# Unread products in the inverse's slots, three trees' bias gathers moved beside the delta rule, tiles added home in two of three segments

## The reference

```python
for _ in range(DEPTH):                       # 8 levels, 256 leaves
    logit = jnp.einsum('bsd,bsd->bs', x, nw[node]) + nb[node]
    node = 2 * node + 1 + (logit > 0).astype(jnp.int32)
leaf = node - NN
h = act(jnp.einsum('bsd,bsdl->bsl', x, w1[leaf]) + b1[leaf])
return jnp.einsum('bsl,bsld->bsd', h, w2[leaf]) + b2[leaf]
```

## Time and profile before

| | |
|---|---|
| median of 3 runs | 4053.92 us (4050.29 to 4074.92) |
| profiled execution: its time, its span | 4069.24 us, 4067.5 us |
| PE busy, over the span | 3332.8 us (82%) |
| DVE, ACT, POOL busy | 2154.1, 1386.8, 918.9 us |
| granted clock of PE, mean over the span | 0.841 |
| PE on the chain that ended last | 64% |
| transfers | 274.44 MB, mean 67 GB/s |

### The profile page before, as it was taken

How to read it: one execution, slowest core, us unless ns; L and a number is a source line. 1 busy time by engine, 2 the same in 40 slices (tenths; PEclk the granted TensorE clock), 3 DMA queues, 4 the chain that set the end, 5 groups by cost and what they waited for, 6 DMA issues and landing times.

```text
span 4067.5 us, 86528 instructions
## 1 busy us (share of the span) xinstructions
PE 3332.8 (82%) x35358; PEld 2395.5 (59%) x35358; DVE 2154.1 (53%) x4781; ACT 1386.8 (34%) x3193; POOL 918.9 (23%) x988
## 2 busy tenths in 40 slices
PE   3488888788887888887676679767599999999998
PEld 3356666566775666666566557556355455545554
DVE  4457677466677566675244345423344554455444
ACT  1344443344344343442033232113144333333331
POOL 0011111411111311113155642345211111101110
PEclk6688897688787888986588889888688999999989
DMA  4201101201001200102174623375310111010000
GB/s 143 101 18 39 34 18 28 99 28 33 28 23 44 89 28 23 34 18 68 43 237 142 199 98 104 111 232 185 136 32 22 42 39 40 22 42 27 16 17 16
DMA packets 202180, 274.44 MB, mean 67 GB/s; under 512 B 33344, under 2 KB 145728, under 8 KB 201408
## 3 DMA queue, kind: packets, MB, share of 16 engines
q1 hardware_dynamic: 174784, 210.04, 16.3%
q0 software_dynamic: 18432, 50.49, 3.5%
...
...
## 4 chain that ended last, share of the span: by engine, by line
PE 64%; DVE 15%; issue 6%; ACT 5%; DMA 3%; another core or an unknown queue 2%; POOL 1%; SPq 0%; DVEq 0%; ACTq 0%; POOLq 0%
PE banks L531 5%; PE banks L2810 5%; DVE s_d_kq L624 3%; PE banks L1781 3%; PE banks L2382 3%; PE banks L1790 2%; PE banks L766 2%; PE banks L2624 2%; PE banks L2366 2%; PE banks L1192 2%; PE banks L755 2%; PE banks L921 2%; PE banks L2394 2%; PE banks L935 2%
## 5 line engine op out<-in xcount | busy, mean ns | idle before, releaser
L531 PE MATMUL banks<-s_d_xT,s_w_qkvg 128*128 128x512 f32 x640 | 353.2, 679 | 30.9 <-DMA s_d_xT<-xnT 21.1
L624 DVE SCALAR_TENSOR_TENSOR s_d_kq<-banks,s_conv_w,s_d_kq 128x511 f32<-128x511 f32 (+2 forms) x384 | 285.7, 745 | 48.5 <-ACT s_d_kq L576 36.9
L2496 ACT ACTIVATE s_g_pT<-banks 128x1536 f32<-128x1536 f32 (+1 forms) x96 | 153.0, 1594 | 436.1 <-PE banks L2384 436.1
L2460 DVE TENSOR_REDUCE s_g_nmax<-banks 128x4 f32<-128x512 f32 (+3 forms) x128 | 187.9, 1489 | 175.5 <-PE banks L2368 175.5
L2810 PE MATMUL banks<-s_m_we,s_m_tT 128*128 128x512 f32 x512 | 233.9, 602 | 3.5 <-DVE s_m_x L2873 3.2
L1781 PEld LDWEIGHTS banks<-s_q_xsT,s_q_w 128*128 128x128 f32 x1008 | 171.7, 216 | 65.0 <-issue 47.0
L1790 PE MATMUL banks<-s_q_w,s_q_hm 128*128 (+1 forms) x504 | 178.7, 442 | 34.5 <-DVE s_q_hm L1834 18.3
L1781 PE MATMUL banks<-s_q_xsT,s_q_w 128*128 x1008 | 174.6, 301 | 37.7 <-issue 30.1
L531 PEld LDWEIGHTS banks<-s_d_xT,s_w_qkvg 128*128 128x128 f32 x640 | 124.1, 213 | 133.9 <-issue 113.4
L602 ACT ACTIVATE s_d_square<-banks 128x128 f32<-128x128 f32 x512 | 134.5, 277 | 191.0 <-PE banks L560 190.9
L1813 ACT ACTIVATE s_q_hT<-banks,s_q_w 128x128 f32<-128x128 f32 x252 | 91.1, 367 | 310.6 <-PE banks L1781 189.5
...
## 6 DMA issues: line engine op xcount, KB each, us to landing
s_q_w<-w12p SPq DMA_DIRECT2D x128, 257.0 KB
...
```

The costliest lines, as they stand in the source:

```text
L531: ins = e.matmul(bk[6 + j % 2][:], w[:, par, c, self.COL[what] + h * P:self.COL[what] + (h + 1) * P], xT[:, c, :], start=(c == 0), stop=(c ...
L624: e.scalar_tensor_tensor(d[:, a:], bk[6 + j % 2][:, 0:SEQ - a], cw[:, par, k0 + 3 - a:k0 + 4 - a], d[:, a:], ALU.mult, ALU.add).then_inc(s ...
L2460: e.tensor_reduce(self.nmax[:, t, :].rearrange("p (k d) -> p k d", k=4)[:, :, 16], psum[:, 0:4, a:a + (t + 1) * P], AX.X, ALU.max, negate= ...
L2496: e.activation(self.pT[c][:], psum[:, 0:4, 0:self.COLUMNS[c]], ACT.Exp).then_inc(self.exped, 1)
```

## The change

1. **Unread products.** `idle_tensor` issues one product of bf16, 128x128 by 128x512, of two constants into bank 3, which nobody reads. It stands in 11 slots of each inversion: behind each T and each Z of the five levels and behind L781, 352 products in all. To make room for later buffers `d_square` becomes bf16. Two semaphores of the inversion are merged.
2. **Biases.** The 96 gathers of trees 0 to 2 leave the segments. Beside the delta rule POOL now gathers each tile's 128 bias rows by token (not by sorted place) into one of two buffers, 23 steps a round behind the leaves, and SP stores the tile into `tree0` to `tree2` with a plain transfer (96 stores of 128 KB). DVE has one more small operation a round (12 in all) that writes the leaf's number as an integer.
3. **Adding home.** In the segments `acc` is set to zero (24 operations of 128x1024 on DVE, `clear`), and the 96 writes become additions to `tree0` to `tree2` (`compute_op` add). They start 35 segments behind the tree's start, not 40, and in trees 0 and 1 stand in two of three segments; in the last tree in each.
4. **Small ones.** The third step of the columns uses a bf16 copy of the leaf column. Tree 3 keeps its gathers and plain writes, waits for gather u-2 in place of u-4, and takes `SCATTER = 35` too.

```diff
@@ Delta.__init__
-        self.square, self.sums = sb("d_square", [P, 2, H, P]), sb("d_sums", [P, 2, TPB * H])
+        self.square, self.sums = sb("d_square", [P, 2, H, P], BF16), sb("d_sums", [P, 2, TPB * H])
@@ invert_tensor, in each of the five levels, after the first and after the second group of products
             ins.then_inc(self.T_made, 1)
             yield
+            self.idle_tensor(e)
             yield
...
             ins.then_inc(self.Z_made, 1)
             yield
+            self.idle_tensor(e)
             yield
         e.wait_ge(self.X_split, m + 1)
-        e.wait_ge(self.X_split2, m + 1)
-        e.wait_ge(self.X_lower, m + 1)
+        e.wait_ge(self.X_split2, 2 * m + 2)
...
             ins.then_inc(self.X_turned, 1)
         yield
+        self.idle_tensor(e)
         yield
...
+    def idle_tensor(self, e):
+
+        e.matmul(self.g.bank[3][:].rearrange("p (h n) -> p h n", h=H), self.g.identb[:], self.g.negm[:, None, :].broadcast_to((P, H, P)), start=True, stop=True)
@@ Routes
-    RT, V, SORT, PLACED = 8, 23, 43, 31
+    RT, V, SORT, PLACED = 8, 24, 43, 31
+        self.leafi, self.bias = sb("leafi", [P, len(trees), TILES], I32), sb("bias", [P, 2, DIM]) if before is None else None
+            self.bias_in, self.bias_out = sems("bias_gathered"), sems("bias_stored")
+    def gather_bias(self, e, F, t):
+        u = TILES * F + t
+        e.wait_ge(self.routed, self.V * (4 * F + t // self.RT + 1))
+        if u >= 2:
+            e.wait_ge(self.bias_out[u % 2], 16 * (u // 2))
+        e.indirect_dma_start(self.bias[:, u % 2, :], None, self.g.dram["b2"], bass.IndirectOffsetOnAxis(self.leafi[:, F, t:t + 1].bitcast(U32), 0)).then_inc(self.bias_in[u % 2], 16)
+
+    def store_bias(self, e, F, t):
+        u = TILES * F + t
+        e.wait_ge(self.bias_in[u % 2], 16 * (u // 2 + 1))
+        e.dma_start(self.g.dram[f"tree{F}"][ds(t * P, P), :], self.bias[:, u % 2, :]).then_inc(self.bias_out[u % 2], 16)
+
+    def beside_biases(self, e, F, steps, one, late):
+
+        for step, _ in enumerate(steps):
+            i, n = divmod(step - self.LEAD - 25 - late, 23)
+            if 0 <= i < self.ROUNDS and n % 2 == 0 and n < 2 * self.RT:
+                one(e, F, self.RT * i + n // 2)
+            yield
+
     def steps_sync(self, e):
+        for F in self.trees:
+            yield from self.beside_biases(e, F, self.tree_sync(e, F), self.store_bias, 3)
...
     def steps_gpsimd(self, e):
         for F in self.trees:
-            for _ in range(self.LEAD + 23 * self.ROUNDS):
-                yield
-            yield from self.seats_gpsimd(e, F)
+            yield from self.beside_biases(e, F, self.tree_gpsimd(e, F), self.gather_bias, 0)
@@ leaves_vector, at the end of a round
+        e.wait_ge(me, v + 23)
+        e.tensor_scalar(self.leafi[:, F - self.trees[0], i * self.RT:(i + 1) * self.RT], self.lf[:, i * self.RT:(i + 1) * self.RT], float(F * LEAVES), None, ALU.add).then_inc(me, 1)
@@ Segments
-    COPIES, SCATTER, GATHER, AHEAD = 6, 40, 46, 3
+    COPIES, SCATTER, CLEAR, AHEAD = 6, 35, 43, 3
+        self.g, self.trees, self.act, self.based = g, trees, act, before is None
+        self.acc_in, self.gathered = routes.bias_in, 16 * len(routes.trees) * TILES // 2
+        self.leafb = [sb(f"leafb{j}", [P, TPB], BF16) for j in range(2)]
@@ columns_tensor, the third step
-                ins = e.matmul(bank[:, t * P:(t + 1) * P], xs[:, t, LEAF:LEAF + 1].broadcast_to((P, P)), self.g.ident[:], start=True, stop=True)
+                ins = e.matmul(bank[:, t * P:(t + 1) * P], self.leafb[b % 2][:, t:t + 1].broadcast_to((P, P)), self.g.identb[:], start=True, stop=True)
@@ vector
+            if self.based:
+                if F == first and n < TILES and n % TPB == 0:
+                    self.clear(e, first, n // TPB)
+                f, due = (Q - self.CLEAR) // SEGS + 1, (Q - self.CLEAR) % SEGS
+                if first < f <= last and due % 6 == 0 and due // 6 < N_BATCH:
+                    self.clear(e, f, due // 6)
+            if self.beside(Q) and self.beside(Q)[2] == 0:
+                self.numbers_vector(e, *self.beside(Q)[:2])
...
+    def clear(self, e, F, b):
+
+        if F > self.trees[0]:
+            for j in range(4):
+                e.wait_ge(self.unsorted[j], 16 * (8 * (F - 1) + b + 1))
+        e.memset(self.acc[:, 4 * b * DIM:4 * (b + 1) * DIM], 0.0).then_inc(self.cleared, 1)
@@ scatter, gather, gpsimd
-        e.indirect_dma_start(self.g.dram[f"tree{F}"], bass.IndirectOffsetOnAxis(self.toki[F % 2][:, t:t + 1].bitcast(U32), 0), self.acc[:, t * DIM:(t + 1) * DIM], None).then_inc(self.unsorted[t % 4], 16)
+        e.indirect_dma_start(self.g.dram[f"tree{F}"], bass.IndirectOffsetOnAxis(self.toki[F % 2][:, t:t + 1].bitcast(U32), 0), self.acc[:, t * DIM:(t + 1) * DIM], None, compute_op=ALU.add if self.based else ALU.bypass).then_inc(self.unsorted[t % 4], 16)
...
-        if u >= 4:
-            e.wait_ge(self.acc_in[t % 4], 16 * (u // 4))
+        if t >= 2:
+            e.wait_ge(self.acc_in[t % 2], self.gathered + 16 * (t // 2))
...
-            if F == first and 2 <= n < TILES + 2:
+            if not self.based and 2 <= n < TILES + 2 and F == first:
                 self.gather(e, first, n - 2)
-            ahead = Q - self.GATHER
-            if ahead >= SEGS * first and ahead // SEGS < last and ahead % SEGS < TILES:
-                self.gather(e, ahead // SEGS + 1, ahead % SEGS)
-            done = Q - self.SCATTER
-            if done >= SEGS * first and done % SEGS < TILES:
-                self.scatter(e, done // SEGS, done % SEGS)
+            f, due = (Q - self.SCATTER) // SEGS, (Q - self.SCATTER) % SEGS
+            if f < last:
+                due = due // 3 * 2 + due % 3 if due % 3 < 2 else TILES
+            if f >= first and due < TILES:
+                self.scatter(e, f, due)
```

93 lines of the change are left out of this document (54 added, 39 removed).

## The result

The changed kernel takes 3963.42 us (median of 4 runs, 3951.5 to 3974.78) beside 4064.42 us for the kernel before in the same comparison (4 runs, 4050.29 to 4077.89): a ratio of 0.9758, 95% interval 0.9734 to 0.9782, 101 us less. (The 4053.92 us of the prediction are the median of the three runs known then.) The profiled execution took 3963.87 us, against 4069.24 before.

A forecast was written before the change was run, and what follows sets the result against it. POOL's queue was taken to bound the slow segments and tail, PE's half-rate clock to slow the delta rule. Segments −90, tree 3 −3, delta rule −10 gave 3966 on the profiled 4069.24, or 3951 us by median; range 3905 to 4000.

The forecast's parts named there:

- POOL no longer back to back: Segments of trees 0 to 2: sign that POOL stopped setting the pace, with stretches of about 57 us for 32 segments.
- the tail begins its 32 writes 5 segments earlier, 3.5: Tail of the segments: writes start earlier but stay one a segment; 5 pieces of 1.28 less PE's need, gaining 3.5 us.
- the slower rival: Segments: adding writes wait for landings and hold POOL and its weight copies; at 12 us a landing about 4115 us; chance 0.05.
- POOL's queue sets these 188 us: Two slow segment stretches: POOL's transfers and weight copies account for 89 of the 95.2 and 93.3 us.
- Cost +40 and gain −57: Delta rule: 352 products take 95 us of PE, 55 hidden; about a fifth of low time removed, 140 us × 0.41.
- the 0.41: Delta rule: share of PE's low-clock time that lengthens the path, from two stretches (0.42) and a line through the others.
- +5 was taken: Delta rule: SP held a little by 96 gathers and stores, plus 12 small DVE operations; +5 us, from 0 to +40.
- −3 was taken: Tree 3: gathers waiting for u−2 cost at most 32 us, earlier writes give 6; −3 us, between −6 and +26.
- The products cost and give nothing: Delta rule: clock stays at 0.81 and products add +40 to +95 us; kernel about 4025 us; chance 0.20.
- The low time is halved: Delta rule: full-array products count for more than small ones, −147 us of clock gain; kernel about 3860 us; chance 0.13.
- All of it goes: Delta rule: pauses alone set the clock, so all 716 us of low time go; kernel at 3712 us; chance 0.03.
- The segments stay held by something else: Segments: loads of weights at 211 GB/s or landings hold them, gaining 45 and not 90; about 4000 us; chance 0.07.

The follow-up runs named there:

- the small products: The changed kernel with each unread product over 32 rows and 32 columns of the array in place of 128 and 128: 4066.5 us, ratio 1.0034.

## Why the prediction was right, point by point

**The sum.** 3951 was forecast for a kernel before of 4053.9; the measured ratio 0.9758 gives 3956 on it. In the profiled execution 105 us went where 103 were forecast. Terms: segments −79 for −90, tree 3 about +1 for −3, delta rule −23 for −10, the rest −4.

That the sum came out so closely is in part luck, since two errors cancel. By the median without products, the rest of the change gives −57 us where the prediction has −88 (−90 − 3 + 5); the products give −35 to −55, depending on the comparison, where it has −17 (+40 − 57). The prediction also said when it would fall: if the delta rule gained over 50 us, or the segments less than 50. In the first pair of profiles they gained 23 and 79, but in the second pair, of the same two kernels, 53 and 43 (1815 to 1762 and 350 to 307). There both signs of being wrong are met, with the same sum.

**The segments.** Half of the mechanism held: POOL's queue is the main limit of the slow stretches, and with its gathers gone they took 52.5 and 48.3 us where 57 was taken and 50 was the lower end. The other half, that PE and the data would then set the pace, did not: the sign for it, "POOL no longer back to back", is missing in the rows after, since 24 adding writes of 1.88 us are 45 us where 22 of 1.28 were 28. That the dearer writes end near the same 50 us as the data's estimate is luck too. How much of the gain comes from the gathers taken away, how much from the writes spread over 48 segments and how much from the columns in bf16, no run tells apart. Three sizes were off. First, the step "the tail begins its 32 writes 5 segments earlier, 3.5": it costed an adding write at a plain one's 981 ns, with nothing in the trace that showed an adding one. It took 1583, and the tail lost 14 us. The bounds for this unknown were only asked for in the slower rival, and there for its landing, not for POOL's own time. Second, the fast stretches lost 6 us where 3 were taken for them and the clearing together. Third, the step "POOL's queue sets these 188 us" named one wait where two stood. POOL's 92 us were there, but 20 of the 112 us for segments 36 to 83 were not POOL's; between the two executions without them the segments gain 43 and not 79 us (350 to 307 in the windows). Counting 89 of 95.2 us hid that: POOL starts 60 of its 64 transfers and 17 copies inside the stretch, which is 84 us, and in the profile without the other waits 50 and 14, in 68.4 us. A length that agrees with a queue's work doesn't show that the queue never waits; POOL's own waits do.

**The delta rule.** Cost +40 and gain −57 were taken. Against the run without products low time fell by 162 us (66 by the 0.41) and the delta rule by 35, so the cost was 31 there; with the kernel before and the products alone it fell by 228 us (93) and the delta rule by 46, so 47 here. If 0.41 is right, the cost of 40 was right, to the 11 us that the rounding of the clocks leaves, and the gain was 9 to 36 us larger than the fifth of the low time that was taken: the removed share was 24 to 35%. Part of that is the prediction's own sum: 76 to 95 of 335 us are 23 to 28%, not a fifth. That the clock would follow idle time filled was the reason given, and it is wrong: the small products filled as much and brought nothing. The row that told better was the one with the same busy 1.21 us and 17 instructions in place of 66. The factor 0.41, from two stretches and a fitted line, is bracketed only through the cost; no run measures it alone.

**POOL and SP beside the delta rule.** +5 was taken. SP waited 406 us for gathers (below) and POOL 103 us for stores, and neither shows in the time beyond the noise: one pair of runs (plain writes, with and without the bias work) puts the gathers and stores at 15 ± 20 us, and the later profiles of the delta rule put them at −8 to +12. SP's waits in the changed kernel's delta rule (us, times, longest), the answer to the earlier trace rows:

```profile
SPq L690 <- DVE s_d_DD L725: 663.3, 31, 60.1
SPq L1165 <- DMA s_r_bias<-b,s_r_leafi: 406.4, 61, 27.8
```

The forecast's sign held: L690's wait went from 890 to 663 us and is still in hundreds. POOL, which reads these loads, didn't wait longer for them either: 224 us before (27 times) and 79 after (13 times).

**Tree 3.** −3 was taken, between −6 and +26, and about +1 came. No run tests this term by itself.

**The rivals.** "The products cost and give nothing" is excluded by the run without them. "The low time is halved" is excluded by 521 of 716 left in the first profiles; in the later ones, with 388 of 653 left, it is not far off, and two products in each slot reach 320. "All of it goes", the pause rule that the prediction took from the Trainium skill, "TensorE: Matmul & The Clock Gate", section "Why this matters for your kernels", would have needed a clock of 1.00: even with 1024 columns in each slot it was 0.91. PE was still idle for 222 us there, so this doesn't test the rule itself; that idle time alone decides is what the small products speak against. "The segments stay held by something else" put their gain at 45: the later profiles have 43, but not for its reason, since POOL's work accounts for 92 of the 92.9 us before, and POOL is back to back after as well. "Slower by adding writes" had the right part of the kernel and the wrong price: break-even was 2.2 us a write, and a write and its wait took 1.85. Its other condition, landings that hold POOL, stood at 1.3 us in all.
